# Decoder layer on one core: attention outputs leave PSUM by ScalarE and are normalised on GpSimd instead of VectorE

## The chip, the cores and the metric

One Trainium2 chip, one core. The metric is device time in microseconds (us). Engines by the names of the profile: PE is TensorE (PEld its weight loads), DVE is VectorE, ACT is ScalarE, POOL is GpSimd, SP the engine that issues most DMAs.

## The reference, cut to what matters

```python
# x: (2, 256, 512); 32 query heads and 8 key/value heads of 16
q, k, v = rope(LN(x) @ Wq), rope(LN(x) @ Wk), LN(x) @ Wv
attn = softmax(causal(q @ k.T / 4))          # per head, 256 x 256
ctx = (attn @ v).reshape(b, t, 512)
x = x + ctx @ Wo
x = x + cross_attention(LN(x), ctx_4096)     # one head of 512, 512 keys
x = x + down(gate(LN(x)) * up(LN(x)))        # ternary weights
```

The change concerns the line with `ctx`: the product with the values is made with unnormalised weights beside a column of ones, so that the sum of the weights (the denominator) comes out of the same product, and the division follows.

## The kernel before, in words

Everything is float32 or a split of it into two parts. The layer norms, the query, key and value projections and the transposes of their stacks come first, up to about 32 us. Then comes a software-pipelined loop over `it` = 0 to 19 for the 16 groups (batch `b`, key/value head `g`, four query heads each). In iteration `it` the engines work on five groups at once:

- group `it`: PE makes the scores by query (L1350 and L1361, eight tiles in banks 0 to 2); DVE takes eight row maxima of them (L980), the first four once PE's four tiles of L1350 are there.
- group `it-1`: PE transposes the maxima (`maxima_T`, L1367), DVE copies them (`mT`, L1050), SP places them with two small DMAs beside the queries.
- group `it-2`: PE makes the scores by key, with the maximum already taken off (L1391, L1397, banks 3 to 5); ACT takes the exponential (L736); POOL clears what the causal mask forbids (L520, two instructions).
- group `it-3`: PE multiplies by the values (`weighted_values`, L1432 and L1436) into the first half of bank 7, for which it waits on `norm_done` of the group before (L1430); ACT copies the result out (`oT`, L746).
- group `it-4`: PE transposes that (`output_T`, L1444) into the second half of bank 7. DVE then makes the reciprocal of the eight denominators per row (L1056) and two products (L1058) into `ctx_tok`, right after its `mT` copy.

Every engine runs its own list in order, and waits on semaphores. Between these steps a table written out by hand (`BESIDE`, three slots per iteration) places the rest of the layer: weight products for the cross attention ("a", L1180), the ternary quantisation of the feed-forward weights ("abs", L573; "whole", L391; "tern", L582), the transposes of the finished rows ("cc", L1087 and L1199), the output projection ("wo", L1211), the norms (stats L767, the power -1/2 on POOL in `root`, L470, then L778), the cross attention ("g", "xs", "xpT", "xo") for batch 0. What matters below:

- "whole" 1, 0 is in slot 2 of iteration 10 and is done by POOL. It needs `inv` of weight 1, which DVE makes in iteration 11 (`scale_of`, L873 to L877, after its `mT` copy and the normalisation).
- "cc" 0 is in slot 1 of iteration 11, ahead of that iteration's `weighted_values`, and waits for the normalised groups 0 to 7 (L1198).
- In iteration 6, slot 2 ends on ACT with the sum of magnitudes ("abs" 1, 0) and "tern" 0, 3. In iteration 16, slot 2 ends on ACT with `xprob` (L589) and the copy of its transpose (L688).
- "cc" 2 is in slot 0 of iteration 19 and needs all 16 groups. Ahead of it POOL has the `root` of "xo" 1, which is in iteration 18.

The list after the loop (`AFTER`) is the rest of batch 1 and the feed-forward layer, mostly PE work, from about 145 us to the end.

Of the kernel before, what the change touches and what calls it, by code (L numbers as in the profile page):

```python
# [10 lines left out]
ALU = mybir.AluOpType  # L11
# [3 lines left out]
P = 128  # L15
B, T, D = 2, 256, 512
# [25 lines left out]
def decoder_layer(nc, x_d, ctx_d, ctxT_d, wqkv_d, wo_d, xwq_d, xwk_d, bq_d, bk_d,  # L42
                  gate_d, up_d, down_d, ident_d, mask_d, rope_d, out_d):
    stack = ExitStack()
    with stack:
        def sb(name, shape, dt=F32, where=stack):
            return where.enter_context(nc.sbuf_tensor(name, shape, dt))
# [8 lines left out]
        def sem(name):  # L56
            return stack.enter_context(nc.semaphore(name))
# [38 lines left out]
        mT = sb("mT", [2 * GROUP, 2, P], F32R)  # L96
        oT = sb("oT", [P, 2, T])
        bkq_term = oT[:, :, :].rearrange("p a q -> p (a q)")
        rden = sb("rden", [P, 2, 2, GROUP])
        part = sb("part", [P, 3, 5])  # L100
        tot = sb("tot", [P, 3])
        scl = sb("scl", [P, 3])
# [88 lines left out]
        smax_ps, max_done, mT_ps, m_sb = sem("smax_ps"), sem("max_done"), sem("mT_ps"), sem("m_sb")  # L191
        sT_ps, exp_done, causal_done = sem("sT_ps"), sem("exp_done"), sem("causal_done")
        pv_ps, pv_sb, oT_ps, norm_done = sem("pv_ps"), sem("pv_sb"), sem("oT_ps"), sem("norm_done")
        abs_done, inv_ready, pool_whole, dve_whole, tern_ready = (
            sem("abs_done"), sem("inv_ready"), sem("pool_whole"), sem("dve_whole"), sem("tern_ready"))
        tot_ready, dve_step = sem("tot_ready"), sem("dve_step")
# [36 lines left out]
        def group(i):  # L233
            b, g = i // KV, PAIRED[i % KV]
            return b, g, g // 2, 64 * (g % 2)
# [225 lines left out]
        @block.gpsimd  # L461
        def _(pool):
            nc.gpsimd.memset(neghalf[:, :], -0.5).then_inc(consts_set, 1)
            nc.gpsimd.memset(ones[:, :], 1.0).then_inc(consts_set, 1)
            nc.gpsimd.memset(vaug[:, :, :, DH:2 * DH], 1.0).then_inc(consts_set, 1)
            pool.wait_ge(consts_set, 3)

            def root(n):
                pool.wait_ge(var_ready, n + 1)
                nc.gpsimd.tensor_tensor(rstd[:, n % 2:n % 2 + 1], veps[:, n % 2:n % 2 + 1],  # L470
                                        neghalf[:, :], ALU.pow).then_inc(rstd_ready, 1)

            for s in range(2):
                nc.gpsimd.memset(stk[:, s, :, 0, :], 0.0).then_inc(stack_set, 1)
            pool.wait_ge(stack_set, 2)
            for s in range(2):
                nc.gpsimd.memset(stk[:, s, HEADS:HEADS + KV, 0, 0:1], -1.0).then_inc(stack_set, 1)
            root(0)
            def w_low(k):
                pool.wait_ge(w_high, k + 1)  # L480
                nc.gpsimd.tensor_tensor(w_lo[:, k, :], wqkv[:, k, :], w_hi[:, k, :].bitcast(F32), ALU.subtract
                                        ).then_inc(w_low_done, 1)

            root(1)
            w_low(0)
            root(2)
            w_low(1)
            pool.wait_ge(xn_ready, 2)
            root(3)
            w_low(2)  # L490
            w_low(3)
            pool.wait_ge(const_in, 16 * 4)
            pool.wait_ge(ident_in, 16)
            nc.gpsimd.memset(maskf[:, 0:P], 0.0).then_inc(bkbc_set, 1)
            nc.gpsimd.tensor_copy(bqbc[:, :, :], bqk[:, 0, :].unsqueeze(2).broadcast_to([P, KD, 32])
                                  ).then_inc(bkbc_set, 1)
            pool.wait_ge(xw_in, 32)
            nc.gpsimd.tensor_scalar(bkq[:, :], xwq[:, 0, :], bqk[:, 1, 0:1], None, ALU.mult).then_inc(bkq_set, 1)
            for k in range(1, KD):
                nc.gpsimd.tensor_scalar(bkq_term, xwq[:, k, :], bqk[:, 1, k:k + 1], None, ALU.mult  # L500
                                        ).then_inc(bkq_set, 1)
                pool.wait_ge(bkq_set, 2 * k)
                nc.gpsimd.tensor_tensor(bkq[:, :], bkq[:, :], bkq_term, ALU.add).then_inc(bkq_set, 1)
                pool.wait_ge(bkq_set, 2 * k + 1)
            def side(pieces):
                for piece in pieces:
                    if piece[0] == "whole":
                        whole(pool, nc.gpsimd, *piece[1:])
                    if piece[0] in ("wo", "xo"):
                        root(norm_no(1 if piece[0] == "wo" else 2, piece[1]))  # L510

            for it in range(NG + 4):
                i = it - 2
                if 0 <= i < NG:
                    pool.wait_ge(exp_done, i + 1)
                    for first in (0, 4 * T):
                        width = T if first == 0 else P
                        v = prob[:, i % 2, first:first + GROUP * width].rearrange(
                            "p (h q) -> p h q", h=GROUP)[:, :, 0:P]
                        nc.gpsimd.affine_select(out=v, in_=v, compare_op=ALU.is_ge, fill=0.0, base=0,  # L520
                                                pattern=[[0, GROUP], [1, P]],
                                                channel_multiplier=-1).then_inc(causal_done, 1)
                side(beside(it, 0) + beside(it, 1) + beside(it, 2))
            side(AFTER)
# [3 lines left out]
        def _(act):  # L528
# [199 lines left out]
            sum_abs(0, 0)  # L728

            for it in range(NG + 4):  # L730
                i = it - 2
                if 0 <= i < NG:
                    act.wait_ge(sT_ps, i + 1)
# [18 lines left out]
        def _(dve):  # L752
# [291 lines left out]
            for it in range(NG + 4):  # L1044
                i = it - 1
                if 0 <= i < NG:
# [1 line left out]
                    if i >= 2:  # L1048
                        dve.wait_ge(m_placed[i % 2], 32 * (i // 2))
                    nc.vector.tensor_copy(mT[:, i % 2, :], ps[0:2 * GROUP, 2, 0:P]).then_inc(m_sb, 1)  # L1050
                i = it - 4
                if 0 <= i < NG:
                    b, g, gp, base = group(i)
                    dve.wait_ge(oT_ps, i + 1)
                    o = ps[:, 7, T:2 * T].rearrange("p (q h e) -> p q h e", q=2, h=GROUP)
                    link(nc.vector.reciprocal(rden[:, i % 2, :, :], o[:, :, :, DH]))  # L1056
                    for q in range(2):
                        nc.vector.tensor_tensor(  # L1058
                            ctx_tok[b][:, q, 4 * DH * g:4 * DH * (g + 1)].rearrange("p (h d) -> p h d", d=DH),
                            o[:, q, :, 0:DH],  # L1060
                            rden[:, i % 2, q, :].unsqueeze(2).broadcast_to([P, GROUP, DH]),
                            ALU.mult).then_inc(norm_done, 1)
                if it in COLUMN_AT:
                    take_column(COLUMN_AT[it])
                side(beside(it, 0))
# [17 lines left out]
        def _(pe):  # L1083
# [74 lines left out]
            def side_products(pieces):  # L1158
                for piece in pieces:
# [35 lines left out]
                                    start=(k == 0), stop=(k == KD - 1), tile_position=(0, 32 * j))  # L1195
                    elif kind == "cc":
                        t = arg[0]
                        pe.wait_ge(norm_done, 2 * KV * (t // 2 + 1))  # L1198
                        mm = transpose_tile(to, ctx_tok[t // 2][:, t % 2, :])  # L1199
                    elif kind == "wo":  # L1200
                        t = arg[0]
# [223 lines left out]
            def weighted_values(i):  # L1425
                b, g, gp, base = group(i)
                pe.wait_ge(causal_done, 2 * (i + 1))
                if i >= 1:
                    pe.wait_ge(pv_sb, i)
                    pe.wait_ge(norm_done, 2 * i)  # L1430
                for h in range(GROUP):
                    nc.tensor.matmul(ps[32 * h:32 * h + 32, 7, 0:T], vaug[:, 2 * b, g, :],  # L1432
                                     prob[:, i % 2, h * T:(h + 1) * T], start=True, stop=False,
# [18 lines left out]
            for it in range(NG + 4):  # L1452
# [11 lines left out]
                if 0 <= it - 3 < NG:  # L1464
                    weighted_values(it - 3)
                side_products(beside(it, 2))
            pe.wait_ge(norm_done, 2 * NG)
            side_products(AFTER)


# [32 lines left out]
```

## Time and profile before

| | us |
|---|---|
| median of 3 runs (234.32 to 235.05) | 234.88 |
| the profiled execution, its own time | 234.35 |
| its span, first to last instruction | 232.3 |
| PE busy | 213.5 (92%) |
| DVE busy | 153.8 (66%) |
| ACT busy | 124.5 (54%) |
| POOL busy | 54.7 (24%) |

The granted TensorE clock was 0.998 of full over the span. Some 2 us of the execution's own time lie outside the span. A row of the timeline gives the start in us from the span's start, how long it took, the engine, the line and operation, what was written and read, how many instructions were merged and, in brackets, how long the engine had been idle and who released it.

### The profile page before, as it was taken

The numbers are of one execution on the slowest core, as the hardware profiler recorded it, in microseconds if no ns is written. First come the engines' busy times: TensorE is split into PE (matmuls) and PEld (weight loads), VectorE is DVE, ScalarE is ACT, GpSimd is POOL, SyncE is SP. The second block draws the span as 40 slices with busy tenths as digits, with TensorE's granted clock in tenths as the row PEclk, the third lists the DMA queues.
The fourth block names the chain that finished last, engine by engine and source line by source line (L and its number), as shares of the span: only waits on it lengthen the run. The fifth ranks groups of instructions, "written<-read, shape, count | busy, mean of one in ns | idle before, by whom it ended". The sixth has DMA issues, their size and how long they took to land.

```text
span 232.3 us, 4242 instructions
## 1 busy us (share of the span) xinstructions
PE 213.5 (92%) x1460; PEld 152.8 (66%) x1468; DVE 153.8 (66%) x560; ACT 124.5 (54%) x209; POOL 54.7 (24%) x72
## 2 busy tenths in 40 slices
PE   8898987998999899999789997999999999999993
PEld 3377866675665565467564544878877878767771
DVE  2489988996888879788522659887355574353233
ACT  2638768785699766078664753737324124322320
POOL 4499920481232442032202030000000010000000
PEclk9999999999999999999999999999999999999999
DMA  6999400001645221167300180000000000020002
GB/s 163 383 396 412 156 1 1 5 1 22 239 144 180 77 67 46 25 247 200 112 1 0 36 329 0 3 0 0 3 1 0 0 3 0 0 93 0 0 3 90
DMA packets 9077, 19.97 MB, mean 86 GB/s; under 512 B 1152, under 2 KB 1536, under 8 KB 9056
## 3 DMA queue, kind: packets, MB, share of 16 engines
q1 hardware_dynamic: 8480, 19.60, 24.4%
q8 instruction: 12, 0.20, 0.3%
q10 hardware_dynamic: 576, 0.10, 0.2%
q14 instruction: 9, 0.07, 0.1%
HBM read 18.58 MB, written 1.05 MB: 85 GB/s over the span
## 4 chain that ended last, share of the span: by engine, by line
PE 65%; ACT 11%; DVE 8%; issue 7%; DMA 6%; SPq 1%; DVEq 0%; POOL 0%; ACTq 0%
PE ps L1289 16%; PE ps L1304 8%; PE ps L1154 7%; PE ps L1227 5%; PE ps L1180 4%; PE ps L1133 4%; PE ps L1211 3%; DMA wqkv<-wqkv_dram 3%; PE ps L1087 3%; DMA raw<-down_dram 3%; PE ps L1350 2%; ACT prob L736 2%; DVE ps L980 2%; ACT gate_q L573 2%; PE ps L1242 2%
## 5 line engine op out<-in xcount | busy, mean ns | idle before, releaser
L980 DVE CUSTOM_DVE_ANT_0 ps<-ps,maskf 128x128 f32<-128x128 f32 (+1 forms) x128 | 41.1, 396 | 0.5 <-PE ps L1350 0.3
L520 POOL TENSOR_SCALAR_AFFINE_SELECT prob<-prob 128x512 f32<-128x512 f32 x32 | 21.1, 683 | 68.8 <-ACT prob L736 68.8
L736 ACT ACTIVATE prob<-ps 128x1536 f32<-128x1536 f32 x16 | 23.3, 1454 | 19.9 <-PE ps L1397 19.7
L605 ACT CAST in_hi<-inter 128x256 f16<-128x256 f32 (+1 forms) x22 | 8.9, 404 | 23.2 <-DVE inter L942 23.2
L470 POOL TENSOR_TENSOR rstd<-veps,neghalf 128x1 f32<-128x1 f32 x12 | 6.6, 553 | 61.5 <-DVE veps L771 61.5
L1289 PE MATMUL ps<-h_hi,gate_q 128*128 128x256 f16 (+1 forms) x88 | 20.4, 273 | 0.0
L1289 PE MATMUL ps<-h_hi,up_q 128*128 128x256 f16 (+1 forms) x88 | 20.4, 273 | 0.0
L1289 PE MATMUL ps<-h_lo,gate_q 128*128 128x256 f16 (+1 forms) x88 | 20.4, 272 | 0.0
L1289 PE MATMUL ps<-h_lo,up_q 128*128 128x256 f16 (+1 forms) x88 | 20.4, 272 | 0.0
L942 DVE TENSOR_TENSOR inter<-gate_s,ps 128x256 f32<-128x256 f32 (+1 forms) x22 | 9.2, 420 | 15.4 <-PE ps L1289 14.7
L980 DVE DVE_READ_ACCUMULATOR2_ANT mx<- 128x1 f32 x128 | 18.5, 144 | 0.0
L598 ACT ACTIVATE gate_s<-ps 128x256 f32<-128x256 f32 (+1 forms) x22 | 8.5, 385 | 18.6 <-PE ps L1289 18.5
L1304 PE MATMUL ps<-wqkv,in_lo 128*128 128x512 bf16 (+1 forms) x44 | 16.7, 379 | 0.8 <-DVE x L952 0.5
L1180 PE MATMUL ps<-xwk,xwq 128*128 128x256 f32 x64 | 16.0, 392 | 0.5 <-ACT qsT L642 0.4
L945 DVE TENSOR_TENSOR in_lo<-inter,in_hi 128x256 f16<-128x256 f32 (+1 forms) x22 | 9.4, 425 | 10.4 <-ACT in_hi L605 10.4
L1227 PE MATMUL ps<-xnT,amat 128*128 128x256 f32 x64 | 14.5, 382 | 1.7 <-ACT gT L680 1.7
L1133 PE MATMUL ps<-ident,stk 128*128 128x128 f32 x80 | 11.5, 281 | 4.0 <-ACT up_q L632 1.3
L1227 PEld LDWEIGHTS ps<-xnT,amat 128*128 128x128 f32 x64 | 12.0, 190 | 3.7 <-ACT gT L680 1.9
L1180 PEld LDWEIGHTS ps<-xwk,xwq 128*128 128x128 f32 x64 | 11.5, 189 | 3.3 <-issue 0.8
L1304 PE MATMUL ps<-wqkv,in_hi 128*128 128x512 bf16 (+1 forms) x36 | 13.6, 379 | 0.0
L1133 PEld LDWEIGHTS ps<-ident,stk 128*128 128x128 f32 x80 | 8.6, 141 | 7.4 <-ACT amat L623 2.6
L1391 PE MATMUL ps<-qsT,ksT 64*128 64x512 f32 x32 | 11.6, 442 | 0.0
(174 smaller groups left out, 511.9 us busy)
## 6 DMA issues: line engine op xcount, KB each, us to landing
raw<-gate_dram SPq DMA_DIRECT2D x1, 2752.0 KB, 17.2
raw<-up_dram SPq DMA_DIRECT2D x4, 688.0 KB, 4.4
wqkv<-wqkv_dram SPq DMA_DIRECT2D x4, 384.0 KB, 6.4
raw<-down_dram SPq DMA_DIRECT2D x2, 768.0 KB, 5.8
x<-x_dram SPq DMA_DIRECT2D x4, 256.0 KB, 5.9
xwq<-xwq_dram SPq DMA_DIRECT2D x1, 1024.0 KB, 9.2
xwk<-xwk_dram SPq DMA_DIRECT2D x1, 1024.0 KB, 11.1
wo<-wo_dram SPq DMA_DIRECT2D x1, 1024.0 KB, 18.0
```

The source lines that it names most:

```text
L520: nc.gpsimd.affine_select(out=v, in_=v, compare_op=ALU.is_ge, fill=0.0, base=0, pattern=[[0, GROUP], [1, P]], channel_multiplier=-1).then_ ...
L736: nc.scalar.activation(prob[:, i % 2, :], ps[:, 3:6, :].rearrange("p a b -> p (a b)"), ACT.Exp, scale=DH ** -0.5).then_inc(exp_done, 1)
L942: nc.vector.tensor_tensor(inter[0:r, n % 2, :], gate_s[0:r, n % 2, :], ps[0:r, 2 + n % 2, 0:T], ALU.mult).then_inc(inter_ready, 1)
L945: nc.vector.tensor_tensor(in_lo[0:r, n % 3, :], inter[0:r, n % 2, :], in_hi[0:r, n % 3, :], ALU.subtract).then_inc(in_lo_ready, 1)
L980: nc.vector.tensor_tensor_reduce(scores, scores, mask, 1.0, LOWEST, ALU.add, ALU.max, to).then_inc(max_done, 1)
L1133: mm = nc.tensor.transpose(to[:, a * P:(a + 1) * P], stk[:, t % 2, h:h + 2, :, :].rearrange("p h c d -> p (h c d)"), ident[:, :])
L1154: mm = nc.tensor.matmul(to, lhs(k), rhs(k), start=(k == 0 and n == 0), stop=(k == KD - 1 and n == 2))
L1180: mm = nc.tensor.matmul(to[:, 0:T], xwq[:, k, m * P:(m + 1) * P], xwk[:, k, half * T:(half + 1) * T], start=(k == 0), stop=(k == KD - 1))
L1227: mm = nc.tensor.matmul(to[:, j * T:(j + 1) * T], amat[:, k, m * P:(m + 1) * P], xnT[:, k, b * T:(b + 1) * T], start=(k == 0), stop=(k == ...
L1289: mm = nc.tensor.matmul(ps[0:r, where + n % 2, 0:T], w[:, k, cols], h[:, k, b * T:(b + 1) * T], start=(k == 0 and h is h_hi), stop=(k == K ...
L1304: mm = nc.tensor.matmul(bank(4 + q), half[0:r, n % 3, q * P:(q + 1) * P], down_q[0:r, it * D:(it + 1) * D], start=(it == 0 and half is in_hi),
L1391: nc.tensor.matmul(bank(3 + n), ksT[rows, gp, b * T:b * T + P], qsT[b][rows, 4 * gp + 2 * n:4 * gp + 2 * n + 2, :], start=True, stop=True)
```

## The change

ACT gets, at the head of each iteration, a copy of the 128 x 256 transposed outputs of group `it-4` from PSUM to a new two-deep buffer `out_tok` in SBUF, signalled by `out_sb`. POOL gets, at the head of each iteration, two instructions: the power -1 of the 128 x 8 denominators in `out_tok`, and one product of 128 x 128 that writes `ctx_tok`. DVE loses its reciprocal and two products. PE waits in `weighted_values` for `out_sb` in place of `norm_done`; "cc" and the end of the loop still wait for `norm_done`, which is now raised once per group. One small constant is set on POOL at the start.

```diff
         @block.gpsimd
             nc.gpsimd.memset(neghalf[:, :], -0.5).then_inc(consts_set, 1)
+            nc.gpsimd.memset(negone[:, :], -1.0)
...
             for it in range(NG + 4):
+                i = it - 4
+                if 0 <= i < NG:
+                    b, g, gp, base = group(i)
+                    pool.wait_ge(out_sb, i + 1)
+                    o = out_tok[:, i % 2, :, :, :]
+                    nc.gpsimd.tensor_tensor(rden[:, i % 2, :], o[:, :, :, DH].rearrange("p q h -> p (q h)"),
+                                            negone[:, :].broadcast_to([P, 2 * GROUP]), ALU.pow).then_inc(rden_done, 1)
+                    pool.wait_ge(rden_done, i + 1)
+                    nc.gpsimd.tensor_tensor(
+                        ctx_tok[b][:, :, 4 * DH * g:4 * DH * (g + 1)].rearrange("p q (h d) -> p q h d", d=DH),
+                        o[:, :, :, 0:DH],
+                        rden[:, i % 2, :].rearrange("p (q h) -> p q h", q=2).unsqueeze(3).broadcast_to([P, 2, GROUP, DH]),
+                        ALU.mult).then_inc(norm_done, 1)
                 i = it - 2
...
         @block.scalar
             for it in range(NG + 4):
+                i = it - 4
+                if 0 <= i < NG:
+                    act.wait_ge(oT_ps, i + 1)
+                    if i >= 2:
+                        act.wait_ge(norm_done, i - 1)
+                    nc.scalar.copy(out_tok[:, i % 2, :, :, :].rearrange("p q h e -> p (q h e)"), ps[:, 7, T:2 * T]
+                                   ).then_inc(out_sb, 1)
                 i = it - 2
...
         @block.vector
-                i = it - 4
-                if 0 <= i < NG:
-                    b, g, gp, base = group(i)
-                    dve.wait_ge(oT_ps, i + 1)
-                    o = ps[:, 7, T:2 * T].rearrange("p (q h e) -> p q h e", q=2, h=GROUP)
-                    link(nc.vector.reciprocal(rden[:, i % 2, :, :], o[:, :, :, DH]))
-                    for q in range(2):
-                        nc.vector.tensor_tensor(
-                            ctx_tok[b][:, q, 4 * DH * g:4 * DH * (g + 1)].rearrange("p (h d) -> p h d", d=DH),
-                            o[:, q, :, 0:DH],
-                            rden[:, i % 2, q, :].unsqueeze(2).broadcast_to([P, GROUP, DH]),
-                            ALU.mult).then_inc(norm_done, 1)
...
         @block.tensor
-                        pe.wait_ge(norm_done, 2 * KV * (t // 2 + 1))
+                        pe.wait_ge(norm_done, KV * (t // 2 + 1))
...
-                    pe.wait_ge(norm_done, 2 * i)
+                    pe.wait_ge(out_sb, i)
...
-            pe.wait_ge(norm_done, 2 * NG)
+            pe.wait_ge(norm_done, NG)
```

## Rows read from the trace of the kernel before

**Rows 1.** The page: the chain that ended last by engine, and ACT's exponential

```profile
PE 65%; ACT 11%; DVE 8%; issue 7%; DMA 6%; SPq 1%; DVEq 0%; POOL 0%; ACTq 0%
...
L736 ACT ACTIVATE prob<-ps 128x1536 f32<-128x1536 f32 x16 | 23.3, 1454 | 19.9 <-PE ps L1397 19.7
```

**Rows 2.** Busy time by stretch: us from and to, length, then each engine's

```profile
100.00:145.00 45.00, 40.16 (x251) 24.82 (x251) 27.13 (x108) 28.24 (x46) 8.77 (x13) 1.00 0.33 111
145.00:232.00 87.00, 82.98 (x560) 64.92 (x566) 46.05 (x105) 31.06 (x70) 2.19 (x4) 1.00 0.04 13
```

**Rows 3.** Groups of instructions, shapes apart: busy us, mean ns, idle before

```profile
L470 POOL TENSOR_TENSOR rstd<-veps,neghalf 128x1 f32<-128x1 f32 x12 | 6.6, 553 | 61.5 <-DVE veps L771 61.5
...
L746 ACT COPY oT<-ps 128x256 f32<-128x256 f32 x16 | 6.0, 373 | 4.4 <-PE ps L1436 4.4
L1058 DVE TENSOR_TENSOR ctx_tok<-ps,rden 128x64 f32<-128x64 f32 x32 | 5.7, 220 | 0.6
...
L1056 DVE RECIPROCAL rden<-ps 128x8 f32<-128x8 f32 x16 | 3.0, 187 | 0.0
...
L495 POOL COPY bqbc<-bqk 128x128 f32<-128x128 f32 x1 | 0.6, 609 | 0.0
```

**Rows 4.** Timeline of iterations 7 to 10: ACT, PE and DVE

```profile
66.76 0.64 PE L1432 MATMUL ps<-prob,vaug 128*32 128x256 f32 x8
...
67.31 1.47 ACT L736 ACTIVATE prob<-ps 128x1536 f32<-128x1536 f32 x1
...
71.19 1.44 ACT L736 ACTIVATE prob<-ps 128x1536 f32<-128x1536 f32 x1
...
74.02 0.27 PE L1350 MATMUL ps<-ksT,qsT 64*128 64x128 f32 x1
...
74.44 0.29 DVE L980 CUSTOM_DVE_ANT_0 ps<-ps,maskf 128x128 f32<-128x128 f32 x1
...
77.80 0.28 DVE L1050 CAST mT<-ps 8x128 fp32r<-8x128 f32 x1
...
78.50 0.29 DVE L980 CUSTOM_DVE_ANT_0 ps<-ps,maskf 128x128 f32<-128x128 f32 x1
```

**Rows 5.** Timeline of iteration 11, around "whole" 1, 0 and "cc" 0

```profile
81.72 0.28 DVE L1050 CAST mT<-ps 8x128 fp32r<-8x128 f32 x1
...
82.42 0.15 DVE L873 TENSOR_SCALAR scl<-ps 128x1 f32<-128x1 f32 x1
...
83.06 1.44 POOL L391 TENSOR_SCALAR raw<-raw,inv 128x1376 f32<-128x1376 f32 x1 [1.99 <-DVE inv L877]
...
83.11 0.66 PE L1087 MATMUL ps<-ident,ctx_tok 128*128 128x128 f32 x4
...
84.43 0.65 POOL L520 TENSOR_SCALAR_AFFINE_SELECT prob<-prob 128x512 f32<-128x512 f32 x1
```

**Rows 6.** Timeline of iteration 17: PE's product with the values, and ACT

```profile
131.33 0.64 PE L1432 MATMUL ps<-prob,vaug 128*32 128x256 f32 x8 [0.29 <-DVE ctx_tok L1058]
131.39 0.58 ACT L688 COPY xprobT<-ps 128x512 f32<-128x512 f32 x1
...
131.86 1.46 ACT L736 ACTIVATE prob<-ps 128x1536 f32<-128x1536 f32 x1
```

**Rows 7.** Timeline of iterations 18 and 19, up to "cc" 2

```profile
141.57 0.59 ACT L675 CAST h_hi<-ps 128x512 f16<-128x512 f32 x1 [0.19 <-PE ps L1087]
...
142.01 0.55 POOL L470 TENSOR_TENSOR rstd<-veps,neghalf 128x1 f32<-128x1 f32 x1 [3.15 <-DVE veps L771]
...
142.60 0.55 DVE L778 TENSOR_SCALAR xn<-x,mv,rstd 128x512 f32<-128x512 f32 x1
...
142.65 0.63 PE L1087 MATMUL ps<-ident,ctx_tok 128*128 128x128 f32 x4 [0.78 <-DVE ctx_tok L1058]
```

**Rows 8.** Timeline: a POOL pair and a DVE instruction that overlaps it

```profile
105.49 1.23 POOL L520 TENSOR_SCALAR_AFFINE_SELECT prob<-prob 128x512 f32<-128x512 f32 x2 [3.26 <-ACT prob L736]
...
106.25 0.75 DVE L778 TENSOR_SCALAR xn<-x,mv,rstd 128x512 f32<-128x512 f32 x1
```

More of the change, by code:

```diff
@@ L98, in decoder_layer @@
         bkq_term = oT[:, :, :].rearrange("p a q -> p (a q)")
-        rden = sb("rden", [P, 2, 2, GROUP])
+        rden = sb("rden", [P, 2, 2 * GROUP])
+        negone = sb("negone", [P, 1])
+        out_tok = sb("out_tok", [P, 2, 2, GROUP, 2 * DH])
         part = sb("part", [P, 3, 5])
@@ L193, in decoder_layer @@
         pv_ps, pv_sb, oT_ps, norm_done = sem("pv_ps"), sem("pv_sb"), sem("oT_ps"), sem("norm_done")
+        out_sb, rden_done = sem("out_sb"), sem("rden_done")
         abs_done, inv_ready, pool_whole, dve_whole, tern_ready = (
```

## The prediction

> **What bounds the kernel now.** I read the chain that ended last first: PE holds 65% of it, ACT 11%, DVE 8% [rows 1]. Then the busy time by stretch: from 145 us to the end PE is busy 83.0 of 87 us, and from 100 to 145 us 40.2 of 45, so what PE loses before 145 us has little slack to vanish in [rows 2]. The change works inside the loop, so I went through the timeline iteration by iteration, and asked of each removed DVE instruction who waited for it, and of each added one what it stands behind in its engine's list and who waits for it.
>
> **What is removed from DVE.** Sixteen reciprocals of 187 ns and 32 products of 220 ns, 3.0 + 5.7 = 8.7 us busy [rows 3], or some 0.5 us of DVE's list per iteration. It is a gain only where DVE's first row maximum waits for DVE and not for PE's fourth score tile. In iteration 9 that tile ends at 74.02 + 0.27 = 74.29 and the maximum starts at 74.44: 0.1 us to gain. In iteration 10 DVE's `mT` copy ends at 78.08 and the maximum starts at 78.50: 0.4 us [rows 4]. In iteration 11 the copy starts at 81.72, and the scaling that follows the three operations at 82.42; without them it starts some 0.2 us after the copy, 0.5 us earlier [rows 5]. At iterations 17 and 19 PE waited for the normalised rows, 0.29 and 0.78 us [rows 6, 7]; both waits get new owners below.
>
> **What ACT gets.** Sixteen copies of 128 x 256 at the head of the iteration; the `oT` copy has the same shape and takes 373 ns [rows 3]. ACT next does the exponential, before which it was idle 19.7 us for PE's scores, by 1.2 us on average [rows 1]. Where it was idle, the copy costs nothing. Where slot 2 of the iteration before keeps ACT busy up to the exponential, two things happen: the exponential is later by up to 0.37 us, and PE's product with the values, which now waits for `out_sb`, stands behind all of that slot.
>
> - Iteration 7: the exponential starts at 67.31, as soon as ACT is free, while PE's product started at 66.76 [rows 4]. The copy would run 67.31 to 67.68, and PE's product follows at about 67.72: PE is 0.96 us later. In iteration 8 ACT has no gap either before its exponential at 71.19 [rows 4], and stays 1.2 us late (0.96, and 0.25 of the copy, since an ACT instruction starts 0.1 before the one ahead of it ends: 131.39 + 0.58 against 131.86 [rows 6]).
> - Iterations 9 and 10: DVE takes 0.1 and 0.4 us back, and is PE's limit there. The `mT` copy at 77.80 follows a sum that ACT delivers, so it is 1.2 us later; the maximum at 78.50 becomes about 79.2, 0.7 later. So iteration 11 begins 0.7 us late.
> - Iteration 17: ACT's list has the copy of the transposed `xprob` (131.39) before the new copy. The exponential followed it at 131.86; now the new copy has that place, to 132.23, and PE's product starts at 132.26 instead of 131.33: **+0.9 us**. PE has no gap behind it that would take this up until iteration 18.
>
> **What POOL gets.** Per group a power of 128 x 8 and a product of 128 x 128, with a wait between them (0.1 us). The nearest row for the power is POOL's own power -1/2 of 128 x 1: 553 ns; for 8 columns that is the low end, and 8 x 553 = 4.4 us the high one, if each column costs all of it. I take 1.0 us, near the row, since a part of 0.55 us must be paid once. For the product the nearest row is a POOL copy of 128 x 128 with a broadcast input, 609 ns [rows 3]; the low end is DVE's two products, 2 x 220 ns, and the high end twice the row. I take 0.6. So the pair costs 1.7 us (1.1 to 5.7). In most iterations it lies beside the exponential of 1454 ns [rows 1] for which POOL's causal instructions wait anyway. It is not covered at two places where PE waits for the normalised rows themselves.
>
> - "cc" 0, iteration 11. In POOL's list "whole" 1, 0 stands ahead of normalisation 7, and it waits for `inv`. It ran from 83.06, and the next POOL instruction started at 84.43 [rows 5]. `inv` moves by +0.7 (above) and -0.5 (no normalisation ahead of it): 83.26 and 84.63. Then 1.0 + 0.1 + 0.6, and PE starts at about 86.37 instead of 83.11: **+3.3 us**. PE has nothing else to do: `weighted_values` and the next product stand behind "cc" 0. The 0.7 of the earlier iterations is in this number, not beside it. With the low ends it is +2.6.
> - "cc" 2, iteration 19. PE transposes group 15; ACT's new copy stands behind its `h_hi` copy of 141.57 and ends at about 142.2. POOL has the root of 142.01 first, some 0.15 us earlier than now, since DVE is freer, so the power starts at 142.39 and PE at 144.13 instead of 142.65 [rows 7]: **+1.5 us** (+0.8 with the low ends).
>
> While this second pair runs, DVE normalises `xn` for the next transposes. An instruction of this kind took 0.75 us where it overlapped a POOL pair from 105.49 to 106.72, and ended 0.28 after it [rows 8]; without overlap the one at 142.60 takes 0.55 [rows 7]. So one of the two would lose some 0.2 us here; I leave it in the range. The Trainium skill (SBUF — State Buffer, "Who interferes with whom") says that such a pair of instructions excludes one another, the second one waiting for all of the first; by that POOL could lose the full 0.55 us and the sum would be 240.5. The trace agrees that the later one is held up, though its 0.2 us are less than a whole instruction.
>
> **At nothing:** the constant on POOL at the start (POOL's first work is far ahead of its users; if uncovered 0.1 us); the remaining waits on `out_sb`, where ACT is ahead; the causal instructions, which now stand behind the pair: PE needs them an iteration later. No DMA is added. SP's queue moves with `mT`.
>
> **Sum** against the profiled execution: 234.35 + 3.3 + 0.9 + 1.5 = 240.0 us. Its time is 0.5 us below the median of the runs, 234.88, so a median for the new kernel might be 240.5. I stay at 240.0.
>
> **Rivals.**
>
> - *A dear power.* If each further column costs two thirds of the first, 0.37 us, it takes 553 + 7 x 370 ns = 3.1 us. Then POOL's list of an iteration is 3.1 + 0.1 + 0.6 + 1.2 (the causal pair [rows 8]) = 5.0 us against iterations of about 4 us in the stretch 7 to 11 [rows 4, 5], and POOL becomes the bound there. From the copy at 67.7 the pairs and causal instructions follow one another, and with "whole" 1, 0 normalisation 7 ends near 93: "cc" 0 is 10 us late; "cc" 2 is 3.6 late. 234.35 + 10 + 0.9 + 3.6 = 249. It decides from a power of about 2.2 us on. For it: one column takes as long as 128 in a copy. Against: that may be a fixed cost. 0.15.
> - *DVE was the bound* (the other side): relief counts, and the new waits are covered, because POOL and ACT get there first. The gains are 0.1 + 0.4 + 0.5 in iterations 9 to 11 and the waits 0.29 and part of 0.78: about 1.5 us, so 232.9. It needs normalisation 7 to be done before 83, so POOL would have to pass "whole" in its list, which is in order. 0.06.
> - *Absorbed:* the delays are taken up by PE's 4.8 us of idle time between 100 and 145 us [rows 2] down to no change, 234.5: 0.04; or by half, 237.3: 0.10. Against: those idle times wait for ACT, which is late with PE.
>
> **How the numbers follow.** The forecast case has 0.65, and with its unknown costs spans 238.7 (low ends) to 243 (a power of 2 us). The range 237.0 to 246.5 takes in this, most of the half-absorbed case and the lower half of the dear power. A measurement can tell about 0.3% from no change. Faster by more than that 0.06, within it 0.04, slower 0.90.
>
> **What would show it.** Right: PE's L1087 on `ctx_tok` in iteration 11 idle for 2 to 3.5 us before it and released by POOL; the same in iteration 19 for about 2 us; the first L1432 of iterations 7 and 17 released by ACT's new copy, about 0.9 us later after its neighbours than before; DVE 8.7 us less busy; POOL some 27 us more. Wrong: a power of over 2 us, POOL without gaps from iteration 7 on, or PE's idle time before L1087 under 1 us.

## The result and the profile after

| | before | after |
|---|---|---|
| median of 4 runs each | 234.94 | 242.78 (242.22 to 243.83) |
| the profiled execution, its own time | 234.35 | 242.22 |
| its span | 232.3 | 240.5 |
| granted TensorE clock over the span | 0.998 | 0.986 |

The kernel is slower by a ratio of 1.0367, 95% interval 1.0336 to 1.0398, some 8 us. The forecast was 240.0, with a range of 237.0 to 246.5, so the median is 2.8 us above it and the profiled execution, the fastest of the four, 2.2.

The page of the changed kernel: busy times, TensorE's clock in 40 slices, the chain by engine, then the groups that are new or have a new wait (busy us, mean ns, idle before them and who ended it).

```profile
PE 215.4 (90%) x1468; PEld 153.9 (64%) x1468; DVE 145.6 (61%) x512; ACT 128.8 (54%) x225; POOL 88.8 (37%) x105
...
PEclk9999999999999959999999999999999999999999
...
PE 63%; ACT 13%; issue 7%; DVE 6%; DMA 5%; POOL 2%; SPq 1%; DVEq 0%; ACTq 0%
...
L522 POOL TENSOR_TENSOR rden<-out_tok,negone 128x8 f32<-128x8 f32 x16 | 28.5, 1783 | 30.0 <-ACT out_tok L753 30.0
...
L525 POOL TENSOR_TENSOR ctx_tok<-out_tok,rden 128x128 f32<-128x128 f32 x16 | 6.4, 401 | 1.3
L753 ACT COPY out_tok<-ps 128x256 f32<-128x256 f32 x16 | 6.1, 381 | 5.2 <-PE ps L1456 5.2
...
L1099 PE MATMUL ps<-ident,ctx_tok 128*128 128x128 f32 x16 | 3.0, 316 | 6.5 <-POOL ctx_tok L525 6.5
```

Against [rows 1] POOL now appears in the chain, and ACT has 2% more of it. The power takes 1.64 us in the median, not 1.0 (the mean of 1.78 has three of sixteen in it that took 1.82, 2.32 and 3.07), the product 0.40, not 0.6, and the transposes of `ctx_tok` (L1087 before, L1099 now) wait 6.5 us in all, in two places. The clock row has one slice at half speed that was not there before.

The timeline at iterations 7 and 8, PE's product with the values (L1432 before, L1444 now) and ACT's new copy (L753):

```profile
66.39 0.38 ACT L753 COPY out_tok<-ps 128x256 f32<-128x256 f32 x1
66.64 1.48 ACT L760 ACTIVATE prob<-ps 128x1536 f32<-128x1536 f32 x1
66.84 1.64 POOL L522 TENSOR_TENSOR rden<-out_tok,negone 128x8 f32<-128x8 f32 x1 [2.46 <-ACT out_tok L753]
...
66.91 0.64 PE L1444 MATMUL ps<-prob,vaug 128*32 128x256 f32 x8 [1.18 <-ACT out_tok L753]
...
71.84 0.42 PE L1444 MATMUL ps<-prob,vaug 128*32 128x256 f32 x4 [0.71 <-ACT out_tok L753]
```

This is PE waiting 1.18 us for a copy that stands behind the whole of slot 2 in ACT's list; in [rows 4] the product had no wait. Its clock time is nearly that of before (66.76), because the front of this execution was 0.9 us shorter; measured from the first transpose of the maxima it is 1.05 us later (66.91 - 33.95 against 66.76 - 34.85). Iteration 11, up to "cc" 0 and the work behind it:

```profile
82.24 0.16 DVE L901 RECIPROCAL inv<-tot 128x1 f32<-128x1 f32 x1
82.50 1.41 POOL L394 TENSOR_SCALAR raw<-raw,inv 128x1376 f32<-128x1376 f32 x1 [0.45 <-DVE inv L901]
83.88 1.63 POOL L522 TENSOR_TENSOR rden<-out_tok,negone 128x8 f32<-128x8 f32 x1
85.59 0.40 POOL L525 TENSOR_TENSOR ctx_tok<-out_tok,rden 128x128 f32<-128x128 f32 x1
...
86.14 1.09 PE L1099 MATMUL ps<-ident,ctx_tok 128*128 128x128 f32 x4 [3.39 <-POOL ctx_tok L525]
...
88.59 3.09 PE L1192 MATMUL ps<-xwk,xwq 128*128 128x256 f32 x8
```

`inv`, "whole", power, product and PE follow one another without a gap, as the forecast had them, and then comes what it did not have: the four transposes take 1.09 us, against 0.66 in [rows 5]. The same stretch by windows (us from and to, length, busy time of PE, its weight loads, DVE, ACT and POOL, granted clock, DMA share, GB/s):

```profile
80.00:86.00 6.00, 2.75 (x44) 1.96 (x36) 4.75 (x28) 2.14 (x4) 5.39 (x8) 0.83 0.28 90
84.00:91.00 7.00, 4.87 (x26) 3.29 (x27) 0.99 (x6) 2.20 (x4) 3.09 (x4) 0.51 0.15 41
86.00:90.00 4.00, 3.87 (x23) 2.48 (x24) 0.00 (x0) 2.19 (x3) 1.16 (x2) 0.50 0.02 4
90.00:93.00 3.00, 3.00 (x20) 2.37 (x18) 0.96 (x2) 0.72 (x3) 0.56 (x1) 0.86 0.00 0
```

From 86 to 90 us the granted clock is 0.50, the lower level of 1.2 GHz. It fell before PE had work again: PE's last product ended at 82.75 (86.14 - 3.39), the clock fell near 84.0, some 1.3 us into the wait, and was back at full near 90.8 (worked out from the means of 0.83, 0.51 and 0.86 over 80 to 86, 84 to 91 and 90 to 93 us). The last two places, iteration 17 and "cc" 2 in iteration 19:

```profile
136.45 0.58 ACT L705 COPY xprobT<-ps 128x512 f32<-128x512 f32 x1
136.91 0.38 ACT L753 COPY out_tok<-ps 128x256 f32<-128x256 f32 x1
...
137.44 0.64 PE L1444 MATMUL ps<-prob,vaug 128*32 128x256 f32 x8 [1.35 <-ACT out_tok L753]
...
148.05 0.55 POOL L474 TENSOR_TENSOR rstd<-veps,neghalf 128x1 f32<-128x1 f32 x1 [1.00 <-DVE veps L795]
148.57 1.64 POOL L522 TENSOR_TENSOR rden<-out_tok,negone 128x8 f32<-128x8 f32 x1
148.63 0.55 DVE L802 TENSOR_SCALAR xn<-x,mv,rstd 128x512 f32<-128x512 f32 x1 [0.67 <-POOL rstd L474]
150.28 0.40 POOL L525 TENSOR_TENSOR ctx_tok<-out_tok,rden 128x128 f32<-128x128 f32 x1
...
150.83 0.63 PE L1099 MATMUL ps<-ident,ctx_tok 128*128 128x128 f32 x4 [3.14 <-POOL ctx_tok L525]
```

**Where the 8.2 us of span went**, from the starts of the same PE instructions in both traces, counted from the first transpose of the maxima (34.85 before, 33.95 after). The rows of that transpose and of the `output_T` behind "cc" 0, before and then after:

```profile
34.85 0.27 PE L1367 MATMUL ps<-ident,mx 128*8 128x128 f32 x1
...
86.45 0.38 PE L1444 MATMUL ps<-ident,oT 128*128 128x128 f32 x2
```

```profile
33.95 0.27 PE L1379 MATMUL ps<-ident,mx 128*8 128x128 f32 x1
...
91.51 0.38 PE L1456 MATMUL ps<-ident,oT 128*128 128x128 f32 x2
```

| PE instruction | before | after | late by | new since the line above |
|---|---|---|---|---|
| maxima of iteration 11 | 46.57 | 47.42 | 0.85 | +0.85 |
| "cc" 0 | 48.26 | 52.19 | 3.93 | +3.08 |
| next `output_T` | 51.60 | 57.56 | 5.96 | +2.03 |
| `output_T` of iteration 17 | 94.80 | 100.75 | 5.95 | 0 |
| `output_T` of iteration 18 | 101.20 | 108.21 | 7.01 | +1.06 |
| "cc" 2 | 107.80 | 116.88 | 9.08 | +2.07 |

9.1 late at "cc" 2, less 0.9 of a shorter front, is the 8.2 of the spans: nothing is lost or won behind "cc" 2. The experiments ask four things: is each of these terms what it is taken for, what does a power cost, is the 2.03 the clock, and is the 0.9 of the front part of the change.

### The profile page after: what moved, and what is told of

The parts are those of the page before. It is cut to its first block, busy times and chain, and to the rows that moved or that the text cites. A ratio compares the mean times of both kernels' runs of the same rounds, so it can differ in the third digit from the quotient of the medians.

```text
span 240.5 us, 4265 instructions
## 1 busy us (share of the span) xinstructions
PE 215.4 (90%) x1468; PEld 153.9 (64%) x1468; DVE 145.6 (61%) x512; ACT 128.8 (54%) x225; POOL 88.8 (37%) x105
## 3 DMA queue, kind: packets, MB, share of 16 engines
HBM read 18.58 MB, written 1.05 MB: 82 GB/s over the span
## 4 chain that ended last, share of the span: by engine, by line
PE 63%; ACT 13%; issue 7%; DVE 6%; DMA 5%; POOL 2%; SPq 1%; DVEq 0%; ACTq 0%
PE ps L1301 16%; PE ps L1316 8%; PE ps L1166 7%; PE ps L1192 5%; PE ps L1239 4%; PE ps L1223 3%; PE ps L1099 3%; PE ps L1270 3%; DMA wqkv<-wqkv_dram 3%; PE ps L1145 3%; DMA raw<-down_dram 3%; ACT prob L760 2%; ACT gate_q L590 2%; PE ps L1254 2%; PE ps L1362 1%
## 5 line engine op out<-in xcount | busy, mean ns | idle before, releaser
L522 POOL TENSOR_TENSOR rden<-out_tok,negone 128x8 f32<-128x8 f32 x16 | 28.5, 1783 | 30.0 <-ACT out_tok L753 30.0
L1192 PE MATMUL ps<-xwk,xwq 128*128 128x256 f32 x64 | 17.0, 412 | 0.4 <-ACT qsT L659 0.4
L1316 PE MATMUL ps<-wqkv,in_hi 128*128 128x512 bf16 (+1 forms) x44 | 16.7, 379 | 0.3 <-DVE x L976 0.3
L1192 PEld LDWEIGHTS ps<-xwk,xwq 128*128 128x128 f32 x64 | 12.3, 202 | 3.7 <-issue 1.2
L1444 PE MATMUL ps<-prob,vaug 128*32 128x256 f32 x128 | 10.7, 405 | 3.5 <-ACT out_tok L753 3.5
```

Source lines behind the costliest of these rows:

```text
L522: nc.gpsimd.tensor_tensor(rden[:, i % 2, :], o[:, :, :, DH].rearrange("p q h -> p (q h)"), negone[:, :].broadcast_to([P, 2 * GROUP]), ALU. ...
L1192: mm = nc.tensor.matmul(to[:, 0:T], xwq[:, k, m * P:(m + 1) * P], xwk[:, k, half * T:(half + 1) * T], start=(k == 0), stop=(k == KD - 1))
L1316: mm = nc.tensor.matmul(bank(4 + q), half[0:r, n % 3, q * P:(q + 1) * P], down_q[0:r, it * D:(it + 1) * D], start=(it == 0 and half is in_hi),
```

## The experiments

Each is the changed kernel with one edit, unless its heading or text says otherwise. Ratios are against the kernel before, timed again beside it (medians of 234.24, 234.16 and 233.49 in the three rounds), so ratios compare better than the times themselves.

### "cc" 0 after the product with the values

```diff
-            ([], [("cc", 0), ("tern", 1, 0)], [("a", 2, 1)]),
+            ([], [("tern", 1, 0)], [("a", 2, 1), ("cc", 0)]),
```

> The changed kernel with one entry of the hand-written table moved: "cc" 0 from slot 1 of iteration 11 to the end of its slot 2, behind the product with the values and "a" 2, 1. Theory (POOL's list makes PE wait 3.4 us at "cc" 0, and the idle time is followed by 6.8 us of a granted clock at the lower level, which costs another 2.0 us in iterations 11 and 12): POOL has the rows ready at about 86.0, when PE comes to "cc" 0, so both the idle time and the low clock go; 242.8 becomes 237 to 238, with the clock at full in the stretch 80 to 100 us. Rival (the loss is spread over the loop by ACT's sixteen copies, and the wait at "cc" 0 only shows where PE meets it): the wait moves to the next product, and less than 2 us are gained, 241 or more.

Measured: 238.41 us, ratio 1.0178 (1.0128 to 1.0229). PE's wait before "cc" 0 fell from 3.39 to 0.68 us and the next `output_T` is 52.70 from the first maxima, 1.1 us later than before instead of 6.0. So some 4.9 us of the profiled loss hang on this one place in PE's list: the wait, and the low clock behind it. The early 0.85, iteration 17 and the tail are untouched. In the tail a new thing shows, first in the timeline and then in two windows:

```profile
146.59 1.09 PE L1099 MATMUL ps<-ident,ctx_tok 128*128 128x128 f32 x4 [3.14 <-POOL ctx_tok L525]
```

```profile
140.00:145.00 5.00, 3.45 (x27) 1.47 (x25) 3.09 (x9) 1.23 (x3) 3.76 (x5) 1.00 0.00 0
145.00:150.00 5.00, 3.41 (x15) 3.19 (x16) 2.21 (x4) 1.32 (x3) 1.37 (x2) 0.66 0.00 0
```

The wait is the same 3.14 us as in the changed kernel, where the transposes behind it took 0.63; here they take 1.09, at the lower level, and the work from "cc" 2 to the end takes 0.8 us more (237.0 - 146.59 against 240.5 - 150.83). That is why the time is above the 237 to 238 that were expected. The clock can fall at either of the two long waits, and in one execution it does and in another it does not.

### A product in place of the power

```diff
-                                            negone[:, :].broadcast_to([P, 2 * GROUP]), ALU.pow).then_inc(rden_done, 1)
+                                            negone[:, :].broadcast_to([P, 2 * GROUP]), ALU.mult).then_inc(rden_done, 1)
```

> The changed kernel with a product in place of the power on POOL, same shapes and waits; the rows come out scaled by minus the denominator and are not normalised. Theory (the power costs 1.64 us for 8 columns, 0.55 of it for the first): the instruction falls to about 0.2 us, the waits at "cc" 0 and "cc" 2 from 3.4 and 3.1 us to about 2.0 and 1.7, that is 2.9 us less; if the clock follows only a longer idle time, another 2.0 us go, so 238 (clock stays full) or 240 (clock still falls). Rival (the wait and the hand-over between the two POOL instructions are the price, not the power): under 1 us gained, 242 or more.

The rows come out unnormalised; only the time is of use. The groups of POOL's two instructions:

```profile
L525 POOL TENSOR_TENSOR ctx_tok<-out_tok,rden 128x128 f32<-128x128 f32 x16 | 7.3, 459 | 1.3
L522 POOL TENSOR_TENSOR rden<-out_tok,negone 128x8 f32<-128x8 f32 x16 | 5.6, 349 | 31.8 <-ACT out_tok L753 31.8
```

The same tile costs 0.35 us as a product and 1.63 as a power, so the power itself is 1.3 us of it (a product had been expected at about 0.2). "cc" 0 came 1.38 us earlier (50.81), and PE's wait there fell from 3.39 to 1.97. Behind it the clock stayed at full, so that the next `output_T` is 2.4 us later than before, not 6.0. The median is 239.88, ratio 1.0212 (1.0136 to 1.0288). So even with a power as cheap as a product the change is some 2% slower, by its other waits. In this execution the clock fell elsewhere, behind PE's waits in iteration 17 and before "cc" 2: 0.57 in each of the windows 134 to 138 and 148 to 152 us.

### The power of 16 columns

The operand is taken with two columns of ones per head, so that 128 x 16 are raised; the rest is as it was.

> The changed kernel with the power over 16 columns (each denominator twice) in place of 8; the product and all waits as they are. Theory (a power costs 0.55 us for one column and (1.64 - 0.55) / 7 = 0.156 us for each further one): 2.9 us for the instruction; POOL's iteration is then 2.9 + 0.1 + 0.4 + 1.2 = 4.6 us, more than the 3.7 to 4.2 us of iterations 8 to 10, so POOL has no gap there and PE's transposes of the maxima 9 to 11 drift by 0.5 to 1 us each; "cc" 0 and "cc" 2 later by 1.3 us or more; 246 to 249. Rival (a fixed cost that steps once above one column): the instruction stays at 1.6 to 1.7 us and the time at 242 to 244.

The group, and POOL's timeline over iterations 9 to 11:

```profile
L522 POOL TENSOR_TENSOR rden<-out_tok,negone 128x16 f32<-128x16 f32 x16 | 49.8, 3111 | 22.1 <-ACT out_tok L753 22.0
```

```profile
80.53 2.90 POOL L522 TENSOR_TENSOR rden<-out_tok,negone 128x16 f32<-128x16 f32 x1
83.50 0.41 POOL L525 TENSOR_TENSOR ctx_tok<-out_tok,rden 128x128 f32<-128x128 f32 x1
83.86 1.22 POOL L537 TENSOR_SCALAR_AFFINE_SELECT prob<-prob 128x512 f32<-128x512 f32 x2
85.07 1.41 POOL L394 TENSOR_SCALAR raw<-raw,inv 128x1376 f32<-128x1376 f32 x1
86.45 2.89 POOL L522 TENSOR_TENSOR rden<-out_tok,negone 128x16 f32<-128x16 f32 x1
```

One execution, 250.45 us, where 246 to 249 were expected. One column takes 0.55 [rows 3], eight 1.64, sixteen 2.90 (the mean of 3.11 has some in it that were held up): about 0.156 us for each column more (1.09 / 7 and 1.26 / 8), on a base of 0.4. And at 2.9 us POOL has no gap left in these iterations: it is the bound, with PE waiting 5.89 us before "cc" 0. That is the rival of the dear power (3.1 us, 249), made real; the change itself, at 1.64, is below the 2.2 us from which the forecast said it decides.

### Work for PE in its wait

Seven products of constants go into the free half of bank 7 while PE would wait; nobody reads them.

```diff
                         t = arg[0]
+                        if t == 0:
+                            pe.wait_ge(out_sb, KV)
+                            for _ in range(7):
+                                nc.tensor.matmul(ps[:, 7, 0:T], ones[:, :], ones[:, :].unsqueeze(1).broadcast_to([P, 2, P]),
+                                                 start=True, stop=True)
                         pe.wait_ge(norm_done, KV * (t // 2 + 1))
```

> The changed kernel, with seven products of ones with 128 x 256 ones on PE ahead of its wait for "cc" 0, into the free half of bank 7. Nothing else moves; PE is busy some 2.7 of the 3.4 us in which it was idle. Theory (the low clock after the wait is caused by the idle time and costs 2.0 us by itself): "cc" 0 starts at the same time, the granted clock stays full, and iterations 11 and 12 are 2.0 us shorter: about 240.8. Rival (the slow instructions from 86 to 91 us come from POOL and ACT working beside PE, or the clock falls on its own): no change, 242.8, with the same 5.4 us from "cc" 0 to the next output transposes.

"cc" 0 and its neighbours in the timeline, and the window behind:

```profile
86.45 0.66 PE L1099 MATMUL ps<-ident,ctx_tok 128*128 128x128 f32 x4
...
87.83 1.99 PE L1192 MATMUL ps<-xwk,xwq 128*128 128x256 f32 x8
```

```profile
86.00:90.00 4.00, 3.90 (x33) 2.61 (x31) 0.00 (x0) 2.33 (x4) 1.58 (x3) 1.00 0.02 4
```

"cc" 0 is where it was (52.13 against 52.19 from the first maxima), so the filling gave PE nothing to get ahead with; what changed is that the transposes take 0.66 and the next product 1.99 instead of 3.09, and the next `output_T` follows 3.21 us behind "cc" 0, not 5.37. So 2.2 us of the profiled loss are the clock alone: the same instructions from the same start, at the lower level in one trace and at full in the other. That the filling is what kept the clock up is not shown. The profiled execution was the fastest of its four, 240.13, with a mean clock of 1.000; the other three had 0.986, 0.978 and 0.986, as low as the changed kernel, so the clock fell in them too, and no trace shows where. With the product in place of the power it stayed at full at this place through an unfilled wait of 1.97 us. The medians say less as well: 241.65 (240.8 expected), ratio 1.0312 (1.0248 to 1.0376), which overlaps the changed kernel's interval.

### "whole" 1, 0 on VectorE

```diff
-        POOL_CHUNKS = [(0, 0), (0, 1), (0, 2), (1, 0)]
+        POOL_CHUNKS = [(0, 0), (0, 1), (0, 2)]
...
-            ([], [], [("whole", 1, 0), ("c",)]),
-            ([], [("cc", 0), ("tern", 1, 0)], [("a", 2, 1)]),
+            ([], [], [("c",)]),
+            ([("whole", 1, 0)], [("cc", 0), ("tern", 1, 0)], [("a", 2, 1)]),
```

> The changed kernel with "whole" 1, 0 given to DVE, at the head of iteration 11, so that nothing stands ahead of normalisation 7 in POOL's list; "cc" 0 stays in slot 1. Theory (half of the wait at "cc" 0 is the order of POOL's list): counted from PE's transpose of the maxima 11, POOL starts the power at about 0.5 us instead of 2.5, and "cc" 0 follows at about 2.7 instead of 4.8; its wait falls from 3.4 to 1.0 to 1.4 us, the clock stays full there, DVE's 1 us of extra work is hidden behind PE: 4 us less than the changed kernel, 238.5 to 239.5. Rival (the power and product alone make the wait, whatever stands ahead): the wait stays over 2.5 us.

```profile
83.94 1.09 PE L1099 MATMUL ps<-ident,ctx_tok 128*128 128x128 f32 x4 [1.53 <-POOL ctx_tok L525]
```

Median 239.53, ratio 1.0256 (1.0209 to 1.0303), 1.1% less than the changed kernel. The profiled execution took 242.67, well above that median, so only its order and its waits are read: POOL's power no longer stands behind `inv` and "whole" but only behind the causal pair, and starts 0.5 us after the copy ends (81.19 and 81.69), PE's wait is 1.53 us instead of 3.39 (1.0 to 1.4 expected), and "cc" 0 is 1.84 us earlier from the first maxima (50.35). So more than half of that wait was `inv` and "whole" standing ahead in POOL's in-order list. In this one execution the clock fell all the same at a wait of 1.53 us (the transposes take 1.09), so a shorter wait is no guarantee. It is not the rule for this kernel either: the mean clock was 0.971 here and 0.984 to 0.993 in the other four executions.

### ScalarE's copy alone

POOL normalises nothing. VectorE makes the reciprocal and one product from `out_tok`, in iterations 4 to 10 and 12 to 15 behind its first side work, in 11 and from 16 on where it did before.

> ACT's copy without POOL's part: DVE normalises out of the copy in SBUF, reciprocal and one product, behind its row maxima; at the head of the iteration only in iteration 11 and from 16 on. Theory (POOL's queue and the power carry the loss, ACT's copies cost the 0.9 us of iteration 17, and up to 0.7 around iterations 7 to 11): no long wait at "cc" 0, the clock full, and 235.5 to 237. Rival (the sixteen copies on ACT carry the loss): 240 or more with the waits on the copy as long as in the changed kernel. If the relief of DVE in its maxima counts for more than thought: below 234.5.

```profile
131.86 0.57 ACT L692 COPY xprobT<-ps 128x512 f32<-128x512 f32 x1
132.32 0.38 ACT L740 COPY out_tok<-ps 128x256 f32<-128x256 f32 x1
...
132.85 0.64 PE L1448 MATMUL ps<-prob,vaug 128*32 128x256 f32 x8 [1.35 <-ACT out_tok L740]
```

235.62 us, ratio 1.0072 (1.0035 to 1.011); clock 1.0 over the span. In the trace the loss is +0.87 by the maxima of iteration 11, +1.06 in iteration 17 (the same 1.35 us wait as above) and +0.2 in the tail. So two of the terms belong to the copy in ACT's list, and the rest of the 8 us to POOL.

### Each group its own way

Three kernels choose the way per group: `d`, VectorE from PSUM as before; `s`, ACT's copy and VectorE from SBUF; `p`, ACT's copy and POOL, as in the change.

```diff
+        WAY = 'sssddssdsssssddd'
...
+        WAY = 'pppddppppppppdpd'
...
+        WAY = 'dddddssddddddddd'
```

The groups 3, 4 and 13, whose copies fall in iterations 7, 8 and 17, are `d` in all three, and so is 15, which "cc" 2 waits for. The second kernel also has "cc" 0 at the end of iteration 11.

> No POOL part. ACT copies the groups 0 to 2, 5, 6 and 8 to 12, and DVE normalises them out of SBUF behind its row maxima; the groups 3, 4, 7, 13, 14 and 15 go the old way, out of PSUM at the head of the iteration. Theory (ACT's copy costs only where its list is full up to the exponential, groups 3, 4 and 13; DVE's relief is worth 0.1 to 0.5 us, in iterations 9 to 11): the waits of PE's product on the copy vanish, the 2.4 us that the copy alone had cost go, and 0.3 to 0.5 us are won against the kernel before: 234.0 to 234.7 where that has 234.5. Rival (any of the copies costs): 235.0 or more.

> POOL normalises as in the change, but not the groups 3, 4, 13 and 15, which go the old way on DVE, and "cc" 0 stands at the end of slot 2 of iteration 11. Theory (the power's 1.64 us are harmless wherever PE has other work until the rows are ready): no wait on POOL or on the copy over 0.5 us, clock full, and the time of the kernel before within 0.5 us: 234.0 to 235.0. Rival (POOL at 37% busy slows DVE by the port they share, or holds back the causal masks): 236 or more, with DVE's or PE's instructions longer than before.

> The kernel before, but ScalarE copies groups 5 and 6 alone out of PSUM and VectorE normalises them from SBUF behind the first side work of its iteration (9 and 10, where the prediction read 0.5 us of relief for VectorE); the other 14 groups go as before, GpSimd normalises none. Theory (the copy in ScalarE costs only where TensorE waits on it, in iterations 7 and 17, and groups 5 and 6 are copied in iterations 9 and 10): no loss at all, and with the front end that all variants had, 233.0 to 233.8, 0.5 to 1.3 us under the kernel before; aligned at the first maxima, cc 0 is 0 to 0.5 us earlier than the 48.26 us of the kernel before. Rival (VectorE isn't what the early queries wait for in these two iterations): aligned, cc 0 at 48.26 and the tail the same to 0.1 us, so that all of the gain is the front end's, 233.5 to 234. If the copies cost something also here, aligned cc 0 is later than 48.3 and the time over 234.3.

Measured, in that order: 233.34, ratio 0.997 (0.9946 to 0.9994); 233.27, ratio 0.9974 (0.9942 to 1.0007); 232.37, ratio 0.9953 (0.9934 to 0.9972). All three are 0.6 to 0.7 us below the low ends of what was expected. So POOL can normalise 12 of the 16 groups, power and all, at no cost that is measured, once no PE instruction stands near behind it. Group 7, with the largest loss, is among these 12: there it was enough to move its reader, "cc" 0. The 8 us therefore sit at five groups: 3 and 4 (iterations 7 and 8), 7, 13 and 15. From the first maxima "cc" 2 is at 107.90, 107.82 and 107.29, against 107.80 before.

The third is below the kernel before by 0.3 to 0.7%. Its trace explains only a part. The maxima of iteration 11 are 0.4 us earlier (46.14 against 46.57), the relief of VectorE that the forecast had read; but "cc" 0 is not (48.21 against 48.26), because of a wait that was hidden before:

```profile
81.26 0.47 PE L1409 MATMUL ps<-ksT,qsT 64*128 64x256 f32 x2 [0.51 <-DVE scl L913]
```

PE's last score tiles now wait for VectorE to take the sum of the magnitudes out of PSUM, which stands behind its normalisation. 0.2 us remain at iteration 15, and 0.5 at "cc" 2; between them lies a wait of PE for ACT's `gT`, 1.35 us here, 1.68 before and 2.00 in the kernel with two buffers more, below, which is as fast as the kernel before. How much of the gain repeats for a reason stays open.

### The kernel before once more, and with two buffers more

The first is the kernel before, unchanged. The second declares the change's two buffers in it and never touches them:

```diff
         rden = sb("rden", [P, 2, 2, GROUP])
+        negone = sb("negone", [P, 1])
+        out_tok = sb("out_tok", [P, 2, 2, GROUP, 2 * DH])
```

> The kernel before, unchanged, profiled a second time. Its first profile has one rope addition of VectorE (L809, 128x512, both operands in SBUF) at 2.75 us beside GpSimd's pair of w_low products (3.67 us), and the first cast of the maxima at 35.16; the changed kernel and all eight variants so far have 0.78 to 0.90 us for that addition, 4.1 us for GpSimd's pair, and every one of them was some 0.3 to 1.4 us earlier at the loop. Theory A (the front end of a program is fixed by the program): 2.75 us and 3.67 us again, to 0.1 us, cast of the maxima within 0.6 us of 35.16. Rival B (which engine is held up there differs from one execution to the next): near 0.8 and 4.1 us. Rival C (the variants gain it by chance of DMA arrival alone): the addition may take either, and the cast's place follows the arrival of x.

> The kernel before with the two SBUF buffers of the change declared and never touched (negone 128x1 and out_tok 128x512 f32, ahead of part, tot and scl), no instruction added or removed. Of the variants, one without the early GpSimd memset had the short front end too, so the memset is not needed for it. Theory A (the addresses of the buffers allocated behind them move, and with them which engine is held up at 15.5 us): the rope addition takes 0.8 to 0.9 us, the first cast of the maxima is near 34.2 instead of 35.16, and the time is 0.4 to 1.0 us under the kernel before, near 233.5. Rival B (addresses don't matter, small shifts of a few hundredths of a microsecond between the two engines decide): 2.75 us as before and a time within 0.2 us of the kernel before, 234.3.

The rope addition in the front and POOL's pair beside it, in the first profile of the kernel before and then in its second:

```profile
14.05 3.67 POOL L481 TENSOR_TENSOR w_lo<-wqkv,qsT 128x768 fp32r<-128x768 f32 x2
15.53 2.75 DVE L809 TENSOR_TENSOR roped<-roped,rope_tmp 128x512 f32<-128x512 f32 x1
```

```profile
14.18 4.13 POOL L481 TENSOR_TENSOR w_lo<-wqkv,qsT 128x768 fp32r<-128x768 f32 x2
15.70 0.89 DVE L809 TENSOR_TENSOR roped<-roped,rope_tmp 128x512 f32<-128x512 f32 x1
```

The same program takes 2.75 us in one execution and 0.89 in the other, and the cast of the maxima starts at 35.16 or 34.56. So the order of the two engines there is a matter of the execution. With the two buffers the addition takes 0.86, as it does without them, and the time is 233.56, ratio 1.0006 (0.9974 to 1.0037): addresses are not needed as a cause and are worth nothing in the time. Of the 0.9 us that the changed kernel's front is shorter by, 0.6 lie between two executions of the unchanged program, so it is not counted as a gain of the change. Its cost in the loop is 9.1 us in the profiled pair, and 7.8 by the medians (234.94 and 242.78); what makes up the rest is open.

## Why the forecast held, and where its terms were off

The direction, the places and the order of the work were right; two sizes and one effect were not. Step by step:

- **"cc" 0, forecast +3.3, measured +3.93.** The mechanism is as written: iteration 11 late by 0.85 (0.7 in the text), then `inv`, "whole", power, product in POOL's list. The failed term is the power, 1.64 us for the 1.0 taken "near the row, since a part of 0.55 us must be paid once": only 0.4 is paid once, and each column adds 0.156, 0.28 of the first. With 0.64 more for it, 0.2 less for the product (0.40, not 0.6) and 0.15 for the iteration, 3.3 becomes 3.9. The bounds of 0.55 and 4.4 did hold it.
- **The clock, forecast nothing, measured +2.03.** This is the largest miss. The forecast priced a wait of PE by its length; the transposes and products behind it ran at 1.2 GHz until about 91 us. The trace with the filled wait shows the price, since the clock stayed at full in it: with "cc" 0 at the same time, the 5.37 us to the next `output_T` become 3.21. When the clock falls is not shown.
- **Iteration 17, forecast +0.9, measured +1.06**, PE released by ACT's copy after 1.35 us, and the copy alone gives the same.
- **"cc" 2, forecast +1.5, measured +2.07** (3.14 us of wait, where about 2 was named as the sign): again the power's 0.64 and the product's 0.2, and 0.1 besides.
- **VectorE's relief.** It is busy 8.2 us less (8.7 forecast; GpSimd 34.1 more, not 27, by its dearer power), worth little, as said: the copies of two groups alone bring the maxima of iteration 11 0.4 us forward and lose it by "cc" 0.
- **The ports in iteration 19**, 0.2 us in the forecast, and up to 0.55 by the rule of the Trainium skill (SBUF — State Buffer, "Who interferes with whom") that it named: the row of `xn` at 148.63 takes its usual 0.55 and the power beside it its 1.64. Neither lost anything, so the rule does not show in this pair.
- **What was costed at nothing** stayed so: between the `output_T` behind "cc" 0 and iteration 17 no time is lost (5.96 against 5.95 late).

The profiled execution took 2.2 us more than the forecast, 242.2 against 240.0. The four terms came to 9.1 us where 5.7 were forecast, 3.4 too little, of which 2.0 are the clock; 0.9 came back by the shorter front of that execution, and 0.3 outside the span. That the result still lies within the case that the forecast gave 0.65 (238.7 to 243) is partly luck: that width was meant for a power of up to 2 us, and the clock, which is in no term, used it. Of the rivals, the dear power is half true: each further column does cost, but 0.156 us and not 0.37, so that POOL does not become the bound of this kernel. "DVE was the bound" and "absorbed" fall with the table above: only 0.2 of the 1.05 us of iteration 7 are won back by iteration 11, and nothing after "cc" 0.

## What to carry to other kernels

Before work goes to an engine with little to do, read what stands ahead of it in that engine's in-order list and which instruction of the bound engine waits right behind it: here 12 of 16 groups moved free once one reader stood later in PE's list, and the 8 us had sat at five groups. Price an operation per element, from rows of two sizes if there are any, before taking a fixed cost for granted. And leave room on top of a wait of TensorE for what its clock may take afterwards, here 2 us at a wait of 3.4 us, and nothing at one of 3.1 in the same execution.

## What the runs showed that was not expected

- **A power on GpSimd is dear by the column:** 0.55, 1.64 and 2.90 us for 1, 8 and 16 columns of 128 partitions, where a product of 128 columns takes 0.40.
- **One wait, two outcomes of the clock.** The tail's 3.14 us of waiting left the clock at full in the changed kernel and was followed by the lower level with "cc" 0 moved; at "cc" 0 it fell within a wait of 1.53 us in one kernel and stayed at full through 1.97 in another. Each is one profiled execution. Mean clocks over the four runs of the changed kernel are 0.986, 0.986, 0.977 and 0.971, for 242.22, 242.99, 242.57 and 243.83 us. What decides it stays open.
- **GpSimd held up for a whole instruction.** In the changed kernel a power lies beside VectorE's pair of L394:

```profile
92.25 1.76 DVE L394 TENSOR_SCALAR raw<-raw,inv 128x1376 f32<-128x1376 f32 x2
92.44 3.07 POOL L522 TENSOR_TENSOR rden<-out_tok,negone 128x8 f32<-128x8 f32 x1 [5.28 <-ACT out_tok L753]
```

The pair ends at 94.01 and the power at 95.51, 1.5 us after, close to its whole 1.64 us: it made almost no progress beside it. The power at 137.38 took 2.32 us beside another such pair and ended 1.49 us after it. The Trainium skill (SBUF — State Buffer, "Who interferes with whom") says that when a VectorE instruction in a mode that takes both of its port pairs, which a `tensor_scalar` can enter, meets one of GpSimd, the one that issues first has the shared pair for its whole length and the other is blocked. The trace agrees here, by the 1.5 us. In the front of both profiles of the kernel before one of the two engines is held up as well, and which one differs (2.75 us for the addition, or 4.13 for GpSimd's pair).
